# Unit samples loaded in 32x32 blocks and transposed by VectorE, unit results stored by GpSimd's queue, splitting of weights respread, 8 idle matmuls

## The chip, the core and the metric

One Trainium2 chip; the kernel runs on one core of it. The metric is device time in microseconds (us) of one execution, the median of several. The core has TensorE (matmuls), VectorE, ScalarE, GpSimd and SyncE, each with an in-order instruction stream of its own; the profile calls them PE (and PEld for its weight loads), DVE, ACT, POOL and SP. Streams wait for one another by semaphores. DMAs are issued by an engine's stream (here SP and POOL, and a few by ACT) and carried out by 16 DMA engines.

## The reference

A batch of 128 samples `x` of 64 rows by 256 columns, in float32. Every sample passes two shared two-layer networks and one of five expert networks, chosen by its integer `itok`; a gate from the samples' first rows mixes the three results; a residual and a stencil step follow. Cut to its core:

```python
def _dense(x, wi_, wo_):
    return jax.nn.relu(x @ wi_) @ wo_            # 256 -> 1024 -> 256
s0, s1 = _dense(x, swi[0], swo[0]), _dense(x, swi[1], swo[1])
h = jax.nn.relu(jnp.einsum('bsd,bdf->bsf', x, wi[itok]))
eo = jnp.einsum('bsf,bfd->bsd', h, wo[itok])
gate_in = jnp.concatenate([eo[:, 0], s0[:, 0], s1[:, 0]], axis=-1)
w = softmax(relu(gate_in @ g1) @ g2)[:, :, None, None]
x = x + eo * w[:, 0] + s0 * w[:, 1] + s1 * w[:, 2]
# then, per sample, with the scalars zX, zY, zR:
x = x + zX * lap_x(x) + zY * lap_y(x) + zR * x * (1 - x)
```

## The kernel before

**Passes and chunks.** The work of TensorE is a row of passes (PASSES), each of 8 chunks of 128 hidden columns. Passes 0 and 1 (PRE) send the samples' first rows through the two shared networks. Passes 2 to 23 (EXP) are 22 expert units: a unit is 8, 4 or 2 samples of one expert, called B, S and T here; pass n does unit n-2, and the order of sizes is BBTBBSBTBSBBTBSBSBTBSB. Which sample stands in which of the 132 slots is worked out on the chip and written into the small table `tab`. Passes 24 to 55 (SH) are 16 tiles of 8 samples times the two shared networks; the gate, the residual and the stencil are done beside them. FIRST is 24.

**A chunk on the engines.** Float32 products are made of split operands: a high part (float32r) by ScalarE and the remainder by VectorE. In step g TensorE does the first product of chunk g (six matmuls with XH, XL and the split weights into `hbank`) and the second product of chunk g-2 (LAG is 2) into `acc`. In between ScalarE makes HH (`hidden_high`, L865) and VectorE HL (`hidden_low`, L528). The second product of a chunk waits for its HL.

**The samples of a unit.** Pass n works on tile n-1. In the pass before, the tile is made ready: SP loads each sample by one DMA into XS (`load_unit_x`, L1023), in rows that lie 8, 4 or 2 partitions apart, having read the sample's number from `tab` (L1010, L1011); TensorE transposes the 128x128 blocks into the PSUM bank `tbank` (`transposes`, L721 to L726); ScalarE takes the high part (`tile_high`, L848, L851) and VectorE the remainder (`tile_low`, L458, L461). For B this is done in two halves, in chunks 3 and 6 (T_ORDER, `tile_parts`). XS has two buffers: the load of tile t waits until tile t-2 has been transposed.

**The tiles of the shared stage** are loaded otherwise: `load_tile_blocks` (L1056) lays 32x32 blocks so that VectorE's transpose, which works within 32x32 blocks, gives the whole transpose at once (`turn_tile`, L471), then `tile_high_whole` (L857) and `tile_low_whole` (L476).

**Weights and results.** GpSimd's stream issues the weights of a unit in four pieces of 512 KB (`load_unit`, L978), each when the raw buffer has been split for the unit before; `cuts_at` is the table that says in which chunk ScalarE splits which piece (L896), VectorE following one chunk later (L561). The unit's results go out by one DMA per sample (`store_unit`, L1033) in SP's stream, in turn with the loads; only half of the last unit's stores are in GpSimd's (L994).

Of the kernel before, what the change touches and what calls it, by code (L numbers as in the profile page):

```python
# [28 lines left out]
WARM = 14  # L29
# [42 lines left out]
def tile_parts(n, c):  # L72

    if n == 0 or n >= FIRST - 1:
        return []
    tile = tile_of(n) + 1
    big = UNITS[tile - 1][1] == 8
    if c == (4 if n == 1 else 3):
        return [(tile, 0 if big else None)]
    return [(tile, 1)] if c == (5 if n == 1 else 6) and big else []  # L80
# [24 lines left out]
def next_tile(n, c):  # L105

    if c != 4 or n < FIRST - 1 or n >= NP - 2:
        return None
    if n == FIRST - 1:
        return 0  # L110
    t, b = PASSES[n][1] // 2, PASSES[n][1] % 2
    return t + 1 if b == 1 else None
# [3 lines left out]


def tile_last(tile):
    return (tile, 1) if (tile, 1) in T_AT else (tile, None)
# [8 lines left out]
def cuts_at(n, c):  # L128
    out = list(FIRST_CUTS.get((n, c), ()))
    at = {2: 0, 4: 2} if 2 <= n < 1 + NU and UNITS[n - 2][1] == 2 else {2: 0, 4: 2, 5: 1, 7: 3}  # L130
    if 2 <= n < 1 + NU and c in at:
        out.append((n + 1, at[c]))

    if 3 <= n <= 1 + NU and UNITS[n - 3][1] == 2 and c < 2:
        out.append((n, 1 + 2 * c))
    return out
# [30 lines left out]
def cond_resid_program(nc, x, itok, zx, zy, zr, wi, wo, swi, swo, g1, g2, out):  # L167
    eo_d = nc.dram_tensor("eo_scratch", (NS + NSLOT, S, D), F32, kind="Internal").ap()
    ctx = ExitStack()
    with ctx:  # L170
# [14 lines left out]
        HF = sb("hf", [128, NH, 128])  # L185
        XS = [sb(f"xs{i}", [128, 4, D]) for i in range(2)]
        EO = [sb(f"eo{i}", [128, 4, D]) for i in range(2)]
        ident = sb("ident", [128, 128])
# [19 lines left out]
        S01 = sb("s01", [128, 2, D])  # L208
# [68 lines left out]
        XB, XZ = RW[0:2], RW[2]  # L277

        def unit_cols(a):
            return a[:].rearrange("p (k n) -> p k n", k=2)  # L280
# [48 lines left out]
        for tile in range(1 + NU + NT):  # L329
            x_slot[tile % 2] += 16 * (slots_of(tile - 1)[1] if 1 <= tile <= NU else 1)  # L330
            X_VAL[tile] = x_slot[tile % 2]
        st_slot = [0, 0]
        ST_VAL = {}
        for u in range(NU):
            st_slot[u % 2] += 16 * slots_of(u)[1] // (2 if u == NU - 1 else 1)
            ST_VAL[u] = st_slot[u % 2]
# [7 lines left out]
        def _(e):  # L344
# [107 lines left out]
            def tile_low(tile, k):  # L452

                hi, lo = unit_cols(XH[tile % 2]), unit_cols(XL[tile % 2])
                e.wait_ge(t_hi, XT_AT[tile, k])
                if k is None:
                    w = S * UNITS[tile - 1][1]
                    e.tensor_tensor(lo[:, :, 0:w], tbank[:, 0:2 * w].rearrange("p (k n) -> p k n", k=2),  # L458
                                    hi[:, :, 0:w].bitcast(F32), ALU.subtract).then_inc(t_free, 1)
                else:  # L460
                    e.tensor_tensor(lo[:, k, :], tbank[:], hi[:, k, :].bitcast(F32),  # L461
                                    ALU.subtract).then_inc(t_free, 1)

            def turn_tile(t):

                if t == 0:
                    e.wait_ge(*cut_done(1 + NU, 2))
                else:
                    e.wait_ge(xt_lo, t)
# [3 lines left out]
            def tile_low_whole(t):  # L473
                tile = 1 + NU + t
                e.wait_ge(xt_hi, t + 1)
                e.tensor_tensor(XL[tile % 2][:], XZ[:], XH[tile % 2][:].bitcast(F32), ALU.subtract).then_inc(xt_lo, 1)  # L476
# [212 lines left out]
        def _(e):  # L689
# [22 lines left out]
            def transposes(tile, k):  # L712
                src = XS[tile % 2]
                e.wait_ge(t_free, T_AT[tile, k] - 1)
                e.wait_ge(x_in[tile % 2], X_VAL[tile])
                if k is None:
                    js = UNITS[tile - 1][1] // 2
                    for kk in range(2):
                        for j in range(js):
                            at = (kk * js + j) * 128  # L720
                            i = e.transpose(tbank[:, at:at + 128], src[:, j, kk * 128:(kk + 1) * 128], ident[:])  # L721
                    i.then_inc(t_prod, 1)
                    return
# [13 lines left out]
            def first_product(g):  # L737
# [16 lines left out]
                if PASSES[n][0] == EXP:  # L754
                    xh, xl = ([unit_cols(a[tile % 2])[:, k, 0:w] for k in range(2)] for a in (XH, XL))
                    to = bank[:, 0:w]
                    if c == 0:
                        e.wait_ge(t_free, T_AT[tile_last(tile)])
                else:
                    xh, xl = ([tile_cols(a[tile % 2], k) for k in range(2)] for a in (XH, XL))  # L760
                    to = bank[:].rearrange("p (j n) -> p j n", j=4)
                    if c == 0:
                        e.wait_ge(xt_lo, PASSES[n][1] // 2 + 1)
# [73 lines left out]
        def _(e):  # L837
# [3 lines left out]
            def tile_high(tile, k):  # L841
                hi = unit_cols(XH[tile % 2])
                e.wait_ge(t_prod, T_AT[tile, k])
                if tile >= 3:
                    e.wait_ge(h_prod, (LAST_PASS[tile - 2] + 1) * NC)
                if k is None:
                    w = S * UNITS[tile - 1][1]
                    e.activation(hi[:, :, 0:w], tbank[:, 0:2 * w].rearrange("p (k n) -> p k n", k=2),  # L848
                                 ACT.Copy).then_inc(t_hi, 1)
                else:  # L850
                    e.activation(hi[:, k, :], tbank[:], ACT.Copy).then_inc(t_hi, 1)  # L851

            def tile_high_whole(t):
                tile = 1 + NU + t
                e.wait_ge(xz_done, t + 1)
                e.wait_ge(h_prod, (LAST_PASS[tile - 2] + 1) * NC)
                e.activation(XH[tile % 2][:], XZ[:], ACT.Copy).then_inc(xt_hi, 1)  # L857
# [40 lines left out]
            def first_samples():  # L898

                e.wait_ge(t_free, T_AT["rows"])  # L900
                e.wait_ge(dve_seq, AT["samples"])
                for b in range(1, 8, 2):
                    e.reg_load(regs[b // 2], tab[0:1, 0, b:b + 1])
                    v = e.snap(regs[b // 2], min_val=0, max_val=NS - 1)
                    e.dma_start(XS[1][b:128:8, :, :], x[bass.ds(v, 1), :, :].rearrange("a (p j) d -> (a p) j d", p=16)) \
                        .then_inc(x_in[1], 16)
# [38 lines left out]
        def _(e):  # L945
# [37 lines left out]
            load_unit(0, (3,))  # L983
            for u in range(1, NU):
                load_unit(u, (0, 2, 1, 3))


            u = NU - 1
            s0, k = slots_of(u)
            e.wait_ge(acc_free, ACC[2 + u, blocks(2 + u) - 1])  # L990
            for b in range(1, k, 2):
                e.reg_load(reg, tab[0:1, 1, s0 + b:s0 + b + 1])
                v = e.snap(reg, min_val=0, max_val=NS + NSLOT - 1)
                e.dma_start(eo_d[bass.ds(v, 1), :, :].rearrange("a (p j) d -> (a p) j d", p=128 // k),  # L994
                            EO[u % 2][b:128:k, 0:k // 2, :]).then_inc(last_out, 16)
# [10 lines left out]
        def _(e):  # L1006
# [6 lines left out]
            def load_unit_x(u, part=None):  # L1013
# [5 lines left out]
                if tile >= 3:  # L1019
# [7 lines left out]
            def store_unit(u, part=None):  # L1027
                s0, k = slots_of(u)
                n = 2 + u
                e.wait_ge(acc_free, ACC[n, blocks(n) - 1])  # L1030
                for b in part or range(k):
                    v = table_value(1, s0 + b, b % 4, NS + NSLOT - 1)
                    e.dma_start(eo_d[bass.ds(v, 1), :, :].rearrange("a (p j) d -> (a p) j d", p=128 // k),  # L1033
                                EO[u % 2][b:128:k, 0:k // 2, :]).then_inc(eo_out[u % 2], 16)

            def load_tile_x(t):
                tile = 1 + NU + t
                if t < 2:
                    e.wait_ge(t_prod, T_AT[tile_last(tile - 2)])
# [4 lines left out]
            def load_tile_blocks(t):  # L1044
# [5 lines left out]
                if t >= 2:  # L1050
                    e.wait_ge(xz_done, t - 1)
# [45 lines left out]
            for u in range(NU):  # L1097
# [6 lines left out]
                if u >= 1:  # L1104
                    store_unit(u - 1)
            store_unit(NU - 1, range(0, slots_of(NU - 1)[1], 2))
# [54 lines left out]
```

## Time and profile before

| | |
|---|---|
| time, median of 3 runs | 1160.17 us (1158.34 to 1160.6) |
| the profiled execution | 1159.52 us, of it 1158.0 us span |
| PE busy | 1135.8 us, 98% |
| DVE / ACT / POOL busy | 675.9 / 453.8 / 72.7 us |
| expert passes, from the first chunk to the first shared chunk | 29.8 to 424.4 us |
| chain that ended last | PE 97%, DVE 1%, DMA 1% |

The first section of the page gives each engine's busy time and its share of the span; the chain of waits is followed back from the last instruction, and tells which engine's work or wait the end hangs on. Instructions that issue DMAs or read registers on SP are not counted as busy; they stand in the timeline as SPq, with the time that each holds SP's stream.

### The profile page before, as it was taken

How to read it: one execution, taken by the hardware profiler on the slowest of the kernel's cores; microseconds unless marked ns; L12 is line 12 of the kernel's file. 1: busy time of each engine (PE TensorE's matmuls, PEld its weight loads, DVE VectorE, ACT ScalarE, POOL GpSimd, SP SyncE). 2: the span in 40 equal slices, each digit the busy share in tenths (PEclk: the TensorE clock that was granted, in tenths of full speed). 3: DMA queues.
4: the chain of work that ended last, by engine and by line, in shares of the span. 5: the costliest groups of instructions: out<-in, count | busy, mean ns of one | idle time of the engine just before them, and what ended most of it. 6: DMA issues, size and time to landing. Idle time of an engine off the chain costs nothing.

```text
span 1158.0 us, 16675 instructions
## 1 busy us (share of the span) xinstructions
PE 1135.8 (98%) x6000; PEld 967.0 (84%) x6000; DVE 675.9 (58%) x1023; ACT 453.8 (39%) x794; POOL 72.7 (6%) x111
## 2 busy tenths in 40 slices
PE   7999999999999999999999999999999999999995
PEld 6788888888888888888888888888888888888884
DVE  6765656656666644546656655655565565465564
ACT  2655545545555532323323333332333333333232
POOL 1111112111111100000000000000000000000001
PEclk9999999999999999999999999999999999999998
DMA  6645456546555514023022022131131231230200
GB/s 216 193 139 179 137 169 183 151 146 184 172 166 153 161 33 118 17 67 83 14 70 74 19 74 41 51 74 29 58 79 21 62 83 20 63 83 15 69 28 28
DMA packets 109986, 107.78 MB, mean 93 GB/s; under 512 B 78320, under 2 KB 86736, under 8 KB 109904
## 3 DMA queue, kind: packets, MB, share of 16 engines
q1 hardware_dynamic: 96832, 60.04, 19.3%
q0 software_dynamic: 12800, 46.41, 13.3%
q8 instruction: 48, 0.79, 0.3%
q10 hardware_dynamic: 272, 0.26, 0.1%
q14 instruction: 34, 0.28, 0.1%
HBM read 85.20 MB, written 17.04 MB: 88 GB/s over the span
## 4 chain that ended last, share of the span: by engine, by line
PE 97%; DVE 1%; DMA 1%; SPq 0%; issue 0%; ACT 0%; DVEq 0%; POOL 0%; POOLq 0%; ACTq 0%
PE acc L793 31%; PE hbank L769 16%; PE hbank L768 16%; PE acc L794 16%; PE hbank L770 16%; PE tbank L725 1%; DMA rw<-in_L_cond_wi 1%; PE acc L694 0%; DMA y<-y 0%; PE tbank L721 0%; PE tbank L726 0%; PE tbank L733 0%; PE acc L782 0%; SPq L1068 0%; DVE ss L599 0%
## 5 line engine op out<-in xcount | busy, mean ns | idle before, releaser
L528 DVE SCALAR_TENSOR_TENSOR hl<-hbank,hh 128x512 fp32r<-128x512 f32 (+2 forms) x432 | 274.2, 636 | 437.1 <-ACT hh L865 436.5
L865 ACT ACTIVATE hh<-hbank 128x512 fp32r<-128x512 f32 (+2 forms) x432 | 238.9, 553 | 597.7 <-PE hbank L770 594.9
L793 PE MATMUL acc<-swo,hh 128*128 128x512 f32 x1024 | 371.0, 397 | 0.0
L794 PE MATMUL acc<-swo,hl 128*128 128x256 f32 x1024 | 286.9, 280 | 0.0
L793 PEld LDWEIGHTS acc<-swo,hh 128*128 128x128 f32 x1024 | 192.4, 188 | 45.3 <-DVE eo L546 0.2
L768 PE MATMUL hbank<-xh,swh 128*128 128x512 f32 x512 | 202.7, 396 | 0.0
L769 PE MATMUL hbank<-xl,swh 128*128 128x512 f32 x512 | 202.4, 395 | 0.0
L794 PEld LDWEIGHTS acc<-swo,hl 128*128 128x128 f32 x1024 | 193.3, 189 | 9.9
L770 PE MATMUL hbank<-xh,swl 128*128 128x512 f32 x512 | 199.4, 389 | 0.0
L793 PE MATMUL acc<-ewo,hh 128*128 128x512 f32 x528 | 194.6, 399 | 0.3
L794 PE MATMUL acc<-ewo,hl 128*128 128x256 f32 x528 | 148.0, 280 | 0.0
L768 PE MATMUL hbank<-xh,ewh 128*128 128x512 f32 (+2 forms) x352 | 124.2, 353 | 0.0
L769 PE MATMUL hbank<-xl,ewh 128*128 128x512 f32 (+2 forms) x352 | 122.3, 347 | 0.0
L770 PE MATMUL hbank<-xh,ewl 128*128 128x512 f32 (+2 forms) x352 | 121.9, 346 | 0.0
L793 PEld LDWEIGHTS acc<-ewo,hh 128*128 128x128 f32 x528 | 99.3, 188 | 22.8 <-DVE hl L528 2.2
L768 PEld LDWEIGHTS hbank<-xh,swh 128*128 128x128 f32 x512 | 96.1, 188 | 23.8
L770 PEld LDWEIGHTS hbank<-xh,swl 128*128 128x128 f32 x512 | 96.4, 188 | 22.3
L769 PEld LDWEIGHTS hbank<-xl,swh 128*128 128x128 f32 x512 | 96.2, 188 | 10.5
L794 PEld LDWEIGHTS acc<-ewo,hl 128*128 128x128 f32 x528 | 99.6, 189 | 4.1
L768 PEld LDWEIGHTS hbank<-xh,ewh 128*128 128x128 f32 x352 | 66.4, 189 | 10.9
L770 PEld LDWEIGHTS hbank<-xh,ewl 128*128 128x128 f32 x352 | 66.4, 188 | 9.5
L769 PEld LDWEIGHTS hbank<-xl,ewh 128*128 128x128 f32 x352 | 66.8, 190 | 4.5
(169 smaller groups left out, 844.5 us busy)
## 6 DMA issues: line engine op xcount, KB each, us to landing
rw<-in_L_cond_wi POOLq DMA_DIRECT2D x44, 512.0 KB, 4.4
rw<-in_L_cond_wo POOLq DMA_DIRECT2D x44, 512.0 KB, 4.6
xs<-in_x SPq DMA_DIRECT2D x128, 64.0 KB, 3.1
eo_scratch<-eo SPq DMA_DIRECT2D x128, 64.0 KB, 2.5
xs<-in_x SPq DMA_DIRECT2D x16, 512.0 KB, 4.2
rw<-in_x SPq DMA_DIRECT2D x256, 32.0 KB, 2.2
ei<-eo_scratch SPq DMA_DIRECT2D x16, 512.0 KB, 5.5
out<-ot SPq DMA_DIRECT2D x15, 512.0 KB, 6.3
```

The costliest lines, as they stand in the source:

```text
L528: e.scalar_tensor_tensor(HL[:, g % NH, 0:w], bank[:, 0:w], 0.0, HH[:, g % NH, 0:w].bitcast(F32), ALU.max, ALU.subtract).then_inc(h_lo, 1)
L725: e.transpose(tbank[:, j * 128:(j + 1) * 128], src[:, j, k * 128:(k + 1) * 128], ident[:])
L768: e.matmul(to, wh[:, k, cs], xh[k], start=(k == 0), stop=False)
L769: e.matmul(to, wh[:, k, cs], xl[k], start=False, stop=False)
L770: i = e.matmul(to, wl[:, k, cs], xh[k], start=False, stop=(k == 1))
L793: e.matmul(acc[j][:, 0:2 * D], HH[:, g % NH, js], woc[:, c, :], start=(c == 0), stop=False)
L794: m = e.matmul(acc[j][:, D:2 * D], HL[:, g % NH, js], woc[:, c, 0:D], start=False, stop=last)
L865: e.activation(HH[:, g % NH, 0:w], hbank[g % HRING][:, 0:w], ACT.Relu).then_inc(h_hi, 1)
```

## The change

- **Loads.** From tile 3 on (the third unit) a sample of a unit is loaded by 4 DMAs of 32 partitions x 4 pieces of 32 columns (128 bytes each), so that the tile lies in 32x32 blocks. Tiles 1 and 2 are still loaded by one DMA a sample and transposed by TensorE, in another layout of rows. The load of tile t waits for VectorE's transpose of tile t-2.
- **Transposes.** From tile 3 on VectorE transposes XS into the new buffer XZ in chunk 3 of the pass before, ScalarE takes the high part of the whole tile from XZ, and VectorE the remainder in chunk 4, as in the shared stage. XZ was a part of the raw weights' buffers; now HF and S01 lie in it.
- **Stores.** All unit results are stored from GpSimd's stream, those of unit u-3 between the second and the third piece of unit u's weights (4 instead of 2 DMAs for a T unit); half of the last unit's are left on SP.
- **Splitting of weights.** `cuts_at`: a T pass splits one piece and leaves three to the next pass's chunks 0, 1, 2; an S pass two and two (chunks 0, 1); a B pass all four, some a chunk later or earlier after a T.
- **Start.** 8 instead of 14 idle matmuls (two rows each in the profile) on TensorE.

```diff
-WARM = 14
+WARM = 8
...
 def tile_parts(n, c):
+    if n == 1 and c in (4, 5):
+        return [(1, c - 4)]
+    return [(2, c // 6)] if n == 2 and c in (3, 6) else []
...
 def next_tile(n, c):
 
-    if c != 4 or n < FIRST - 1 or n >= NP - 2:
+    if c != (3 if n < FIRST - 1 else 4) or n < 3 or n >= NP - 2 or (n >= FIRST and PASSES[n][1] % 2 == 0):
         return None
...
+    return tile_of(n) + 1
...
+    if 2 <= n < 1 + NU:
+        size = UNITS[n - 2][1]
+        late = 3 <= n and UNITS[n - 3][1] == 2
+        at = {2: 0} if size == 2 else {2: 0, 4: 2} if size == 4 else {3 if late else 2: 0, 5 if late else 4: 2,
+                                                                      6 if late else 5: 1, 7: 3}
+        if c in at:
+            out.append((n + 1, at[c]))
+    if 3 <= n <= 1 + NU:
+        at = {2: {0: 2, 1: 1, 2: 3}, 4: {0: 1, 1: 3}, 8: {}}[UNITS[n - 3][1]]
+        if c in at:
+            out.append((n, at[c]))
...
+            def turn_tile(tile):
+
+                if XZ_AT[tile] > 1:
+                    e.wait_ge(xt_lo, XZ_AT[tile] - 1)
+                if tile <= NU:
                     w = S * UNITS[tile - 1][1]
...
+                    e.wait_ge(x_in[tile % 2], X_VAL[tile])
+                    e.transpose(XZ[:, 0:2 * w], XS[tile % 2][:].rearrange("p j d -> p (j d)")[:, 0:2 * w]) \
+                        .then_inc(xz_done, 1)
+                    return
...
+            def tile_low_whole(tile):
+                w = width(LAST_PASS[tile])
+                e.wait_ge(xt_hi, XZ_AT[tile])
+                e.tensor_tensor(XL[tile % 2][:, 0:2 * w], XZ[:, 0:2 * w], XH[tile % 2][:, 0:2 * w].bitcast(F32),
+                                ALU.subtract).then_inc(xt_lo, 1)
...
+            def tile_high_whole(tile):
+                w = width(LAST_PASS[tile])
+                e.wait_ge(xz_done, XZ_AT[tile])
                 e.wait_ge(h_prod, (LAST_PASS[tile - 2] + 1) * NC)
-                e.activation(XH[tile % 2][:], XZ[:], ACT.Copy).then_inc(xt_hi, 1)
+                e.activation(XH[tile % 2][:, 0:2 * w], XZ[:, 0:2 * w], ACT.Copy).then_inc(xt_hi, 1)
...
+            def store_unit(u, part=1):
+                s0, k = slots_of(u)
+                e.wait_ge(acc_free, ACC[2 + u, blocks(2 + u) - 1])
+                for i, (b, g) in enumerate(stores(u)[::part]):
+                    e.reg_load(targets[i % 4], tab[0:1, 1, s0 + b:s0 + b + 1])
+                    v = e.snap(targets[i % 4], min_val=0, max_val=NS + NSLOT - 1)
+                    to, of = store_ends(u, b, g, v)
+                    e.dma_start(to, of).then_inc(eo_out[u % 2], 16)
+
+            e.wait_ge(dve_seq, AT["targets"])
             for u in range(1, NU):
-                load_unit(u, (0, 2, 1, 3))
...
+                load_unit(u, (0, 2))
+                if u >= 3:
+                    store_unit(u - 3)
+                load_unit(u, (1, 3))
...
-                if tile >= 3:
-                    e.wait_ge(t_prod, T_AT[tile_last(tile - 2)])
+                if tile in (3, 4):
+                    e.wait_ge(t_prod, T_AT[tile - 2, 1])
+                if tile >= 5:
+                    e.wait_ge(xz_done, XZ_AT[tile - 2])
+                to = XS[tile % 2][:].rearrange("p j d -> p (j d)")[:, 0:128 * k].rearrange("p (c b n) -> p c b n", c=4, b=k)
                 for b in part or range(k):
                     v = table_value(0, s0 + b, b % 4, NS - 1)
-                    e.dma_start(XS[tile % 2][b:128:k, 0:k // 2, :],
-                                x[bass.ds(v, 1), :, :].rearrange("a (p j) d -> (a p) j d", p=128 // k)) \
-                        .then_inc(x_in[tile % 2], 16)
...
+                    rows = sample.rearrange("a (r g) (k d) -> (a r) (g k) d", g=2, k=2)
+                    for q in range(4):
+                        qs = slice(32 * q, 32 * q + 32)
+                        e.dma_start(to[qs, :, b, :], rows[:, :, qs]).then_inc(x_in[tile % 2], 16)
...
-                if u >= 1:
-                    store_unit(u - 1)
```

How the instructions stand now, at three places. First SP's stream at the load of a sample from tile 4 on. Before, two samples (TENSOR_LOAD reads the sample's number, ISA works out the address):

```order
L1010 TENSOR_LOAD tab
L1011 ISA
L1023 DMA xs<-in_x 16x1024
L1010 TENSOR_LOAD tab
L1011 ISA
L1023 DMA xs<-in_x 16x1024
```

Now, one sample and the head of the next:

```order
L1053 DMA xs<-in_x 32x4x32
L1053 ISA
L1053 DMA xs<-in_x 32x4x32
L1053 ISA
L1053 DMA xs<-in_x 32x4x32
L1053 ISA
L1053 DMA xs<-in_x 32x4x32
L1028 TENSOR_LOAD tab
L1029 ISA
```

Where one DMA stood there are four, with an address instruction ahead of each of the three further ones.

Second, VectorE around chunk 3 of pass 4 (the first T pass), where tile 4 (a B tile) is made ready; `hl<-hbank` is the hidden remainder of a chunk, `ewl<-rw` a split of weights. Before:

```order
L528 SCALAR_TENSOR_TENSOR hl<-hbank1,hh 128x128
L461 TENSOR_TENSOR xl0<-tbank,xh0 128x512
L528 SCALAR_TENSOR_TENSOR hl<-hbank2,hh 128x128
L561 TENSOR_TENSOR ewl1<-rw0,ewh1 128x2x512
L528 SCALAR_TENSOR_TENSOR hl<-hbank0,hh 128x128
```

Now:

```order
L549 SCALAR_TENSOR_TENSOR hl<-hbank1,hh 128x128
L486 STREAM_TRANSPOSE xz<-xs0 128x1024
L549 SCALAR_TENSOR_TENSOR hl<-hbank2,hh 128x128
L582 TENSOR_TENSOR ewl1<-rw0,ewh1 128x2x512
L496 TENSOR_TENSOR xl0<-xz,xh0 128x1024
L549 SCALAR_TENSOR_TENSOR hl<-hbank0,hh 128x128
```

Between the HL of chunk 2 and that of chunk 3 stands the transpose of the whole tile, and the whole remainder stands ahead of the HL of chunk 4; both stood as halves, the second half in chunk 6.

Third, GpSimd's stream: before, the four pieces of a unit's weights stood alone. Now, with three of the eight stores of a B unit:

```order
L987 DMA rw<-in_L_cond_wo 128x4x256
L999 TENSOR_LOAD tab
L1000 ISA
L1002 DMA eo_scratch<-eo 64x1x256
L999 TENSOR_LOAD tab
L1000 ISA
L1002 DMA eo_scratch<-eo 64x1x256
```

The third and the fourth piece (L987) come after the last of these stores.

## Rows read from the trace of the kernel before

**Rows 1.** First section of the page: busy time (share of span) and instructions
```profile
PE 1135.8 (98%) x6000; PEld 967.0 (84%) x6000; DVE 675.9 (58%) x1023; ACT 453.8 (39%) x794; POOL 72.7 (6%) x111
```
**Rows 2.** Two windows: us, busy (instructions) PE, PEld, DVE, ACT, POOL, clock, DMA, GB/s
```profile
1.50:3.00 1.50, 1.50 (x7) 1.50 (x8) 0.36 (x3) 1.28 (x1) 1.08 (x5) 1.00 0.47 103
...
30.00:424.40 394.40, 392.69 (x2228) 339.65 (x2227) 242.60 (x367) 208.69 (x363) 61.11 (x83) 1.00 0.53 158
```
**Rows 3.** TensorE's timeline: the first shared chunk
```profile
424.44 0.39 PE L768 MATMUL hbank<-xh,swh 128*128 128x512 f32 x1
```
**Rows 4.** SP's timeline: a B unit's loads (start us, us)
```profile
103.17 7.46 SPq L1023 DMA_DIRECT2D xs<-in_x  x8
```
**Rows 5.** TensorE's transposes of unit samples: durations ns min/median/max, first and last start
```profile
L725 PE MATMUL tbank<-ident,xs x78: 270/272/328, 24.1 to 400.4; 128*128 128x128 f32 x78
L721 PE MATMUL tbank<-ident,xs x28: 270/272/273, 61.3 to 375.8; 128*128 128x128 f32 x28
L726 PE MATMUL tbank<-ident,xs x26: 272/272/273, 24.5 to 400.5; 128*128 128x128 f32 x26
```
**Rows 6.** The chain in order of time (start us, us, what), pieces of several windows
```profile
1.48 5.33 PE acc L694 x28
...
47.09 0.33 PE tbank L725 x3
...
80.85 0.33 PE tbank L725 x3
...
84.35 0.33 PE tbank L725 x3
...
395.68 0.33 PE tbank L725 x3
396.00 0.11 PE tbank L726
...
400.33 0.33 PE tbank L725 x3
```
**Rows 7.** The chain in the window 14 to 20: one sample on SP
```profile
16.21 0.28 SPq L1010
...
16.53 0.04 SPq L1011
...
16.67 0.50 SPq L1023
17.17 0.04 issue
```
**Rows 8.** What a DMA holds SP: all unit samples; a T unit's (window 123:126); shared blocks, landing
```profile
L1023 SPq DMA_DIRECT2D xs<-in_x x128: 472/495/753, 15.5 to 378.5; - x128
...
L1023 SPq DMA_DIRECT2D xs<-in_x x2: 550/551/552, 123.5 to 124.6; - x2
...
L1056 SPq DMA_DIRECT2D rw<-in_x x16: 577/608/647, 487.1 to 497.2; - x16
...
DMA to landing us min/median/max: 2.1/2.2/2.4
```
**Rows 9.** Groups by line and form: count | busy us, mean ns of one | idle before
```profile
L471 DVE STREAM_TRANSPOSE rw<-rw 128x1024 f32<-128x1024 f32 x16 | 19.8, 1238 | 3.2 <-DMA rw<-in_x 3.2
L476 DVE TENSOR_TENSOR xl<-rw,xh 128x1024 fp32r<-128x1024 f32 x16 | 19.5, 1216 | 0.0
L857 ACT ACTIVATE xh<-rw 128x1024 fp32r<-128x1024 f32 x16 | 17.0, 1063 | 50.9 <-DVE rw L471 50.9
L528 DVE SCALAR_TENSOR_TENSOR hl<-hbank,hh 128x256 fp32r<-128x256 f32 x40 | 16.8, 420 | 13.9 <-ACT hh L865 13.9
L865 ACT ACTIVATE hh<-hbank 128x256 fp32r<-128x256 f32 x40 | 15.3, 384 | 24.0 <-PE hbank L770 23.4
```
**Rows 10.** GpSimd's timeline: the first and the last of its four stores
```profile
432.52 0.53 POOL L994 DMA_DIRECT2D eo_scratch<-eo  x1 [38.35 <-issue]
...
435.78 0.48 POOL L994 DMA_DIRECT2D eo_scratch<-eo  x1 [0.42 <-issue]
```

More of the change, by code:

```diff
@@ L105, in next_tile @@
 def next_tile(n, c):
-    if c != 4 or n < FIRST - 1 or n >= NP - 2:
+    if c != (3 if n < FIRST - 1 else 4) or n < 3 or n >= NP - 2 or (n >= FIRST and PASSES[n][1] % 2 == 0):
         return None
[L109 to L112, printed above, removed]
+    return tile_of(n) + 1
+XZ_AT = {}
+for _n, _c in CHUNKS:
+    if next_tile(_n, _c) is not None:
+        XZ_AT[next_tile(_n, _c)] = len(XZ_AT) + 1
 LAST_PASS = {tile_of(n): n for n in range(NP)}
-def tile_last(tile):
-    return (tile, 1) if (tile, 1) in T_AT else (tile, None)
 FIRST_CUTS = {(0, 4): [(0, 0)], (0, 5): [(0, 2)], (0, 6): [(0, 1)], (0, 7): [(0, 3)], (1, 3): [(2, 0)], (1, 6): [(2, 2)],
@@ L329, in cond_resid_program, with stores, store_ends @@
         for tile in range(1 + NU + NT):
-            x_slot[tile % 2] += 16 * (slots_of(tile - 1)[1] if 1 <= tile <= NU else 1)
+            x_slot[tile % 2] += 16 * (slots_of(tile - 1)[1] * (1 if tile <= 2 else 4) if 1 <= tile <= NU else 1)
             X_VAL[tile] = x_slot[tile % 2]
+        def stores(u):
+            return [(b, g) for b in range(slots_of(u)[1]) for g in ((0, 1) if slots_of(u)[1] == 2 else (None,))]
+        def store_ends(u, b, g, v):
+            ps, js = unit_rows(u, b, g or 0)
+            to = eo_d[bass.ds(v, 1), :, :].rearrange("a (r g) d -> (a r) g d", g=2)
+            return to if g is None else to[:, g:g + 1, :], EO[u % 2][ps, js, :]
         st_slot = [0, 0]
@@ L334, in cond_resid_program @@
         for u in range(NU):
-            st_slot[u % 2] += 16 * slots_of(u)[1] // (2 if u == NU - 1 else 1)
+            st_slot[u % 2] += 16 * len(stores(u)) // (2 if u == NU - 1 else 1)
             ST_VAL[u] = st_slot[u % 2]
@@ L715, in transposes @@
                 e.wait_ge(x_in[tile % 2], X_VAL[tile])
[L716 to L723, printed above, removed]
                 for j in range(3):
@@ L754, in first_product @@
                 if PASSES[n][0] == EXP:
[L755 to L758, printed above, removed]
+                    xh, xl = ([unit_cols(a[tile % 2], k, w) for k in range(2)] for a in (XH, XL))
+                    to = bank[:, 0:w].rearrange("p (g n) -> p g n", g=2)
+                    if c == 0 and tile <= 2:
+                        e.wait_ge(t_free, T_AT[tile, 1])
+                    elif c == 0:
+                        e.wait_ge(xt_lo, XZ_AT[tile])
                 else:
@@ L983, in _ @@
             load_unit(0, (3,))
-            for u in range(1, NU):
-                load_unit(u, (0, 2, 1, 3))
[L988 to L995, printed above, removed]
+            targets = [e.alloc_register(f"target{k}") for k in range(4)]
+            def store_unit(u, part=1):
[7 more added lines that the diff above has]
+            e.wait_ge(dve_seq, AT["targets"])
+            for u in range(1, NU):
+                load_unit(u, (0, 2))
+                if u >= 3:
+                    store_unit(u - 3)
+                load_unit(u, (1, 3))
+            store_unit(NU - 3)
+            store_unit(NU - 2)
+            store_unit(NU - 1, 2)
             t = NT - 1
```

92 lines of the change are left out of this document (35 added, 57 removed).

## The prediction

> **What bounds the kernel now.** I read the busy times first. TensorE is busy for 1135.8 of 1158.0 us [rows 1], and the chain that ended last is TensorE for 97% (the table). So one asks of every edit only whether TensorE has less to do, or comes to wait. Then the expert passes as a window: from 30.0 to 424.4 us TensorE is busy for 392.7 of 394.4 us, VectorE for 242.6, ScalarE for 208.7, GpSimd for 61.1 [rows 2]. Nothing but TensorE's work sets the length of this stage, and the shared stage behind it, from 424.44 us on [rows 3], isn't touched but for its first tile. The whole question is when the first shared chunk starts.
>
> SP is in none of these shares, since an instruction that issues a DMA isn't counted as busy. Its timeline has to be read: the eight loads of a B unit hold its stream for 7.46 us [rows 4], so a sample costs (7.46 - 0.50)/7 = 0.99 us. With 116 loads from the third unit on and nearly as many stores that is about 230 us of the stage's 394: SP has room. This is the number that the change moves most.
>
> **What TensorE is spared.** It transposes 78 + 28 + 26 = 132 blocks [rows 5]; the 16 of tiles 1 and 2 stay, 116 go. Their durations overlap; on the chain four of them take 0.33 + 0.11 = 0.44 us [rows 6], 0.11 each. Sum: 12.8 us, all on the path, as nothing else bounds it there. The idle matmuls: 28 rows take 5.33 us from 1.48 us on [rows 6], the first ones 1.50/7 = 0.214 us each [rows 2]. The 16 that are left end at 1.48 + 3.42 = 4.9 us instead of 6.8, and the table of slots, on which the first weights wait, follows: 1.9 us. If the slower pace of the first rows then lasts longer, a part is given back, at worst all 5.33 us that the idle matmuls took; between -1.9 and +5 us, and I take -1.9. With no new wait at all the profiled execution would be 1159.5 - 14.7 = 1144.8 us.
>
> **What SP has to do now.** Stores leave it (they cost 116 us of a stream that wasn't bound, so nothing). A load becomes four DMAs. The anatomy of one sample before [rows 7]: from the address instruction to the DMA 0.14 us (16.53 to 16.67), behind it 0.04 us, and the reading of the number in front. The three further DMAs each bring an address instruction and themselves: 0.18 + d, where d is what such a DMA holds the stream. The first costs 0.50 + d, by the 0.99 us above with d = 0.495. A sample is 1.04 + 4d.
>
> d isn't in the trace. The rows around it [rows 8]: the lowest of all unit loads 0.472 us (no loads by register are cheaper), 64 pieces of 1 KB by register 0.551 us, and the shared tiles' blocks, 32 partitions x 8 pieces of 128 bytes at constant addresses, 0.608 us. The new DMA has the form of the last with half the pieces, and an address from a register; the bounds are 0.47 (the lowest row) and 0.68 (the highest, and on it the 0.08 by which small pieces by register exceed the lowest). I take 0.58, between the two nearest rows. A sample then costs 3.36 us, a B unit 26.9, an S unit 13.4, a T unit 6.7.
>
> TensorE needs less: three chunks of an S pass take 400.33 - 395.68 - 0.44 = 4.21 us and three of a T pass 84.35 - 80.85 - 0.44 = 3.06 us [rows 6], so 1.40 and 1.02 a chunk, and a B chunk, with twice an S chunk's columns, 2.79; a B pass is about 20 to 22 us. SP falls behind by up to 5 us with each B unit. Only two buffers lie between them, so it becomes the bound.
>
> The ledger. Tile 4, from which SP is never idle again by these numbers, may be loaded when the second half of tile 2 is transposed, before at 47.09 + 0.44 = 47.5 us [rows 6], now 45.6. From there 22 tiles less three, 114 samples x 3.36 = 383.0 us: tile 22, the last, is issued at 428.6 us. Its landing takes 2.2 us [rows 8]. Then, in pass 22 (S), stand in line VectorE's transpose 1.24, ScalarE's high part 1.06 and hidden high part 0.38, VectorE's hidden remainder 0.42, a split of weights and the remainder of the tile 1.22 each, and the hidden remainder of chunk 4, 0.42 [rows 9]: 5.96 us, to 436.8. There TensorE goes on with the second product of chunk 4, which stands 3 x 1.40 + 0.70 = 4.9 us behind the start of chunk 3. From the start of chunk 3 to the first shared chunk it took 424.44 - 395.68 - 0.88 (two transposes) = 27.9 us [rows 3, 6], so 23.0 are left: the first shared chunk starts at 459.8 us, 35.4 later than before. The first shared tile's 16 DMAs at 0.65 us (0.608 + 0.04) follow tile 22 and are there before chunk 4 of pass 23. The sum against the execution's own time: 1159.5 + 35.4 = 1194.9 us; that execution lies 0.7 us below the median of the runs, which is less than I can tell, so 1195.
>
> The Trainium skill, in DMA: Bandwidth & Descriptors, "Issuing engines are not separate DMA queues", says that the time on the sequencer to start a DMA is "usually small relative to the DMA itself". By that rule the queue wouldn't bound and the time would be that of the first rival below; the trace disagrees for these pieces, as four of 16 KB would each hold the stream for 0.76 us where the old one of 64 KB held it for 0.99 in all.
>
> **The other edits.** Results through GpSimd: its stores lie (435.78 - 432.52)/3 = 1.09 us apart [rows 10], so eight hold back the third and fourth piece of weights by 8.7 us, about three B chunks. A store of unit u-3 isn't needed before pass u. The pieces come about a pass ahead, so I cost it at nothing while SP stretches the passes; without that, up to 2 us behind each of the four T units, 8 in all. VectorE's added transposes (11 B, 5 S, 4 T tiles, at most 1.24 each: 17 us) fit into its 150 idle us, except where they stand ahead of a hidden remainder in a short pass (below). The respread splitting moves no work; it keeps four splits of 1.22 us out of a T pass of 10 us. I cost it at nothing.
>
> **The rivals.** First, SP keeps up: d is at or below 0.47, a sample at or below 2.93 us. Then tile 22 is issued by 45.6 + 334 = 379.6 us, ahead of chunk 3 of its pass, and the time is 1145 us, the full 14.7 gained. For it: one row at 0.472. Against it: all rows with small pieces are above 0.55. This is the other side.
>
> Second, SP keeps up, but the gain goes into the new line through VectorE and ScalarE in the short passes. In a T pass it is, from the start of chunk 3, 0.3 (VectorE comes to it late by a hidden remainder) + 1.24 + 1.06 + 0.28 + 0.29 + 1.22 + 1.22 + 0.29 = 5.9 us to the remainder of chunk 4, against 3 x 1.02 + 0.67 = 3.7 in which TensorE needs it: 2.2 us, four times. In an S pass 6.3 against 4.9: 1.3 us, five times. (The 128-column forms are taken as two thirds of the 256-column ones.) Together 15 us, so 1160 us: no change. The line holds whether or not SP is late; with SP late it is hidden but for the last, which the ledger has.
>
> Third, SP bound and dearer: d = 0.608 gives 3.47 us a sample, 1159.5 + 48 = 1207; d = 0.68 gives 1240. Cheaper: 0.551 gives 1182. Every 0.01 us of d is 4.6 us of time. Fourth, the transfers don't do what they should: pieces of 128 bytes beside the weights land late. With 2.2 us landing against a pass of lead this costs a few us at most, and it is in the range.
>
> **How the numbers follow.** SP bound with d from 0.52 to 0.64, the forecast and what lies around it (1166 to 1222 us): 0.62. Dearer still: 0.10. SP keeps up, with the gain kept or partly kept (1145 to 1157): 0.18. SP keeps up or nearly, with nothing gained: 0.10, most of it within 0.2%. The likeliest case's own range is 1170 to 1220. The range that holds 8 in 10 reaches down to 1150 and up to 1226. About 0.2% (2.3 us) is what a measurement of this kernel can tell from no change: faster 0.20, within it 0.07, slower 0.73.
>
> **What would show it.** Right: in the changed profile SP's stream has no idle time between the loads from tile 4 to 22; a B unit holds it for about 27 us; VectorE's transpose of unit tiles is what TensorE's chain passes through, with the loads (DMA, SPq) as its releaser, tiles 5, 11, 12, 16, 18 and 22 most; TensorE is busy for some 14 us less and idle for some 50 us in the expert passes, and the shared stage is as long as before. Wrong: SP waits for VectorE's transposes (then it kept up), or TensorE's waits end on ScalarE's high part without a late DMA (second rival), or on weights whose DMA GpSimd issued behind its stores; or the time is under 1165.

## The result and the profile after

The changed kernel takes 1204.3 us, median of 4 runs (1202.88 to 1207.21), against 1160.38 us (1158.34 to 1160.71) before: ratio 1.0385, interval 1.0362 to 1.0409. It is slower by 44 us; the prediction said 1195 us, slower with a chance of 0.73. The page of the changed kernel, busy times and chain:

```profile
PE 1143.8 (95%) x5872; PEld 969.2 (81%) x5872; DVE 690.6 (57%) x1032; ACT 451.1 (38%) x783; POOL 141.2 (12%) x243
...
PE 64%; SPq 28%; issue 5%; DMA 1%; DVE 1%; ACT 0%; DVEq 0%; POOL 0%; ACTq 0%; POOLq 0%
SPq L1053 24%; PE acc L808 21%; PE acc L809 11%; PE hbank L783 11%; PE hbank L784 11%; PE hbank L785 10%; SPq L1028 3%; SPq L1029 0%; DMA xs<-in_x 0%; DMA rw<-in_L_cond_wi 0%; PE acc L715 0%; DMA y<-y 0%; PE tbank L746 0%; PE acc L797 0%; PE hbank L763 0%
```

Where TensorE had 97% of the chain, SP's issuing has 28% of it now. The expert stage as a window up to the first shared chunk, which answers to the second row of [rows 2] and to [rows 3] (the columns are those of rows 2):

```profile
30.00:468.38 438.38, 398.97 (x2106) 340.78 (x2105) 255.87 (x376) 205.68 (x351) 129.55 (x215) 0.95 0.54 141
```

The first shared chunk starts at 468.38 us instead of 424.44, 43.9 later, and from there to the end of the span it takes 733.8 us (before 733.6): all of the loss lies in the expert stage. TensorE is idle for 39.4 us of it (before 1.7). And it is *busy* for 6.2 us more than before, though it transposes 116 blocks fewer: the granted clock of the window is 0.95 instead of 1.00. The two sum to the 43.9.

The line of the loads and their landing; SP's timeline over 12 samples (start us, us):

```profile
L1053 SPq DMA_DIRECT2D xs<-in_x x457: 563/563/1835, 39.9 to 432.4; - x153
...
DMA to landing us min/median/max: 1.9/2.7/6.6
```
```profile
204.97 40.48 SPq L1053 DMA_DIRECT2D xs<-in_x  x48
```

One of these DMAs holds SP for 563 ns, a sample for 40.48/12 = 3.37 us where it took 0.99. A merged row of SP's timeline would hide idle time, so the row itself doesn't show that there is none; the sum does: 12 samples by the prediction's formula with d = 0.563 are 39.5 of the 40.5 us. In the trace no two neighbouring instructions of SP lie more than 0.4 us apart from the first load of tile 4 (46.26 us) to the last issue. SP never catches up. Who waited, on VectorE and on TensorE (us in total, times, longest):

```profile
DVE xz L486 <- DMA xs<-in_x: 30.6, 5, 9.3
```
```profile
PE acc L808 <- DVE hl L549: 32.7, 15, 7.3
PE acc L808 <- DVE ewo L582: 4.7, 4, 1.2
```

VectorE's transpose waits five times for a tile, 30.6 us in all: for tiles 5, 11, 12, 18 and 22, five of the six that the prediction named (16 came in time). TensorE's waits are put down to the hidden remainder (L549), which stands behind that transpose in VectorE's stream; the DMA is found one step further back. The longest of the five in windows of TensorE (columns as in rows 2):

```profile
234.00:238.00 4.00, 4.00 (x22) 3.37 (x21) 0.59 (x1) 0.00 (x0) 1.23 (x2) 1.00 0.62 154
238.00:242.00 4.00, 2.19 (x11) 1.49 (x10) 0.00 (x0) 0.00 (x0) 0.00 (x0) 1.00 0.50 149
242.00:246.00 4.00, 0.00 (x0) 0.00 (x0) 1.25 (x1) 0.84 (x1) 0.00 (x0) 0.53 0.12 19
246.00:250.00 4.00, 2.52 (x8) 2.15 (x9) 3.27 (x4) 3.56 (x6) 0.71 (x1) 0.50 0.14 21
250.00:254.00 4.00, 4.00 (x16) 3.29 (x15) 2.56 (x4) 0.60 (x1) 1.30 (x2) 0.69 0.84 165
```

TensorE stands still from about 240 to 247 us; the granted clock falls to half (0.50: 1.2 of 2.4 GHz) in the stall and is still there while TensorE works again: 22 matmuls in a full window at 1.00, 16 in the one at 0.69. Whether that is paid for depends on what is late next: where the next tile comes late anyway, a slower TensorE only waits less.

The end of the stage: SP's last loads, VectorE's last unit transpose, TensorE behind it.

```profile
425.83 7.14 SPq L1053 DMA_DIRECT2D xs<-in_x  x9
```
```profile
437.98 1.25 DVE L486 STREAM_TRANSPOSE xz<-xs 128x1024 f32<-128x1024 f32 x1 [5.14 <-DMA xs<-in_x]
```
```profile
441.10 0.79 PE L808 MATMUL acc<-ewo,hh 128*128 128x512 f32 x1 [4.91 <-DVE hl L549]
```

The last issue ends at 432.97, the tile is there 5.0 us later, and the first matmul behind it takes 0.79 us instead of 0.4.

### The profile page after: what moved, and what is told of

Read it like the earlier page. It is cut to its first block, busy times and chain, and to the rows that moved or that the text cites. A ratio compares the mean times of both kernels' runs of the same rounds, so it can differ in the third digit from the quotient of the medians.

```text
span 1202.2 us, 17512 instructions
## 1 busy us (share of the span) xinstructions
PE 1143.8 (95%) x5872; PEld 969.2 (81%) x5872; DVE 690.6 (57%) x1032; ACT 451.1 (38%) x783; POOL 141.2 (12%) x243
## 4 chain that ended last, share of the span: by engine, by line
PE 64%; SPq 28%; issue 5%; DMA 1%; DVE 1%; ACT 0%; DVEq 0%; POOL 0%; ACTq 0%; POOLq 0%
SPq L1053 24%; PE acc L808 21%; PE acc L809 11%; PE hbank L783 11%; PE hbank L784 11%; PE hbank L785 10%; SPq L1028 3%; SPq L1029 0%; DMA xs<-in_x 0%; DMA rw<-in_L_cond_wi 0%; PE acc L715 0%; DMA y<-y 0%; PE tbank L746 0%; PE acc L797 0%; PE hbank L763 0%
## 5 line engine op out<-in xcount | busy, mean ns | idle before, releaser
L549 DVE SCALAR_TENSOR_TENSOR hl<-hbank,hh 128x512 fp32r<-128x512 f32 (+2 forms) x432 | 273.6, 636 | 456.7 <-ACT hh L873 456.2
L808 PE MATMUL acc<-ewo,hh 128*128 128x512 f32 x528 | 202.9, 413 | 38.0 <-DVE hl L549 32.7
L808 PEld LDWEIGHTS acc<-ewo,hh 128*128 128x128 f32 x528 | 102.5, 194 | 64.3 <-DVE hl L549 36.5
L809 PE MATMUL acc<-ewo,hl 128*128 128x256 f32 x528 | 151.1, 286 | 0.0
L784 PE MATMUL hbank<-xl,ewh 128*128 128x512 f32 (+2 forms) x352 | 125.9, 358 | 0.0
L785 PE MATMUL hbank<-xh,ewl 128*128 128x512 f32 (+2 forms) x352 | 125.3, 356 | 0.0
L809 PEld LDWEIGHTS acc<-ewo,hl 128*128 128x128 f32 x528 | 103.1, 195 | 4.2
L1002 POOL DMA_DIRECT2D eo_scratch<-eo x136 | 69.5, 511 | 96.4 <-issue 84.2
L783 PEld LDWEIGHTS hbank<-xh,ewh 128*128 128x128 f32 x352 | 69.8, 198 | 13.1
```

Source lines behind the costliest of these rows:

```text
L549: e.scalar_tensor_tensor(HL[:, g % NH, 0:w], bank[:, 0:w], 0.0, HH[:, g % NH, 0:w].bitcast(F32), ALU.max, ALU.subtract).then_inc(h_lo, 1)
L783: e.matmul(to, wh[:, k, cs], xh[k], start=(k == 0), stop=False)
L784: e.matmul(to, wh[:, k, cs], xl[k], start=False, stop=False)
L785: i = e.matmul(to, wl[:, k, cs], xh[k], start=False, stop=(k == 1))
L808: e.matmul(acc[j][:, 0:2 * D], HH[:, g % NH, js], woc[:, c, :], start=(c == 0), stop=False)
L809: m = e.matmul(acc[j][:, D:2 * D], HL[:, g % NH, js], woc[:, c, 0:D], start=False, stop=last)
```

## Experiments

The theory after this reading: the loss is SP's issuing of four DMAs a sample (A). What was open: whether the number of DMAs, their duration, or the small pieces and their late landing decide it; what the other edits cost once SP keeps up; and what the clock adds.

**One DMA a sample, in before's form.** All other edits stay.

```diff
-                    for q in range(4):
-                        e.dma_start(to[qs, :, b, :], rows[:, :, qs])...
+                    e.dma_start(XS[tile % 2][b:128:k, 0:k // 2, :],
+                                sample.rearrange("a (p j) d -> (a p) j d", p=128 // k))...
...
```

> The changed kernel, but from tile 3 on each unit sample is loaded by one DMA in the form of the kernel before (pieces of 4, 2 or 1 KB); all waits, VectorE's transposes, GpSimd's stores and the table of splits stay. The rows are not laid out for a 32x32 transpose, so the values of the expert passes are other ones. Theory (SP's issuing bounds the expert passes): SP needs 0.99 us a sample instead of 3.4, VectorE never waits for xs, and about 50 us of the 44 lost and 15 gained come back: 1145 to 1157 us, the first shared chunk at 410 to 422 us. Rival 1 (the new line through VectorE and ScalarE in S and T passes costs as much as the transposes did): 1160. Rival 2 (GpSimd's queue holds the weights back and is what TensorE waits for): stays above 1190.

Measured: 1171.83 us (ratio 1.0101, 1.0086 to 1.0117). The stage, and TensorE's waits:

```profile
30.00:436.22 406.22, 388.77 (x2103) 332.49 (x2102) 254.75 (x374) 205.32 (x350) 129.14 (x215) 0.98 0.51 151
```
```profile
PE acc L808 <- DVE hl L549: 10.8, 13, 1.2
PE acc L808 <- DVE ewo L582: 4.7, 4, 1.2
```

32.5 us of the 44 go with the three further DMAs: A holds for them. But the time lies in neither expected range (1145 to 1157, or 1160): the kernel is still 12 us slower than before where 14.7 us of gain were due. SP isn't waited for any more, and yet TensorE is idle for 17.4 us, and busy for 9.5 us longer than in the version further down whose clock never falls in this window (379.3). Here the granted clock is at half for 17.1 us of the window, in four stretches, one in each T pass. So there are further causes, of 27 us together.

**Four DMAs with one piece of 512 bytes a partition.** The same number of DMAs, bytes and partitions, larger pieces.

```diff
-                        e.dma_start(to[qs, :, b, :], rows[:, :, qs])...
+                        e.dma_start(whole[qs, 128 * b:128 * b + 128],
+                                    rows[:, q:q + 1, :].rearrange("r o d -> r (o d)"))...
```

> The changed kernel with its four DMAs a sample, each to 32 partitions by register as now and of the same 16 KB, but in one piece of 512 bytes a partition instead of four of 128. The pieces land in another arrangement, so the values of the expert passes are other ones. Theory (the number of issues on SP bounds): d stays at 0.50 to 0.57 us, the loads end at 410 to 433 us and the time is 1180 to 1205. Rival (it is the pieces of 128 bytes that make the transfers slow and late): 1145 to 1165, as with one DMA a sample.

Measured: 1171.44 us (1.0072 to 1.0105). What a DMA holds SP:

```profile
L1054 SPq DMA_DIRECT2D xs<-in_x x464: 315/316/1468, 33.9 to 393.7; - x155
```

The expectation that d stays near 0.5 us failed: it is 0.316. So the run doesn't separate pieces from issuing as it was meant to. It shows something else: the count of DMAs alone doesn't bind, but the count times what each holds SP for. By the prediction's formula a sample is 1.04 + 4 x 0.316 = 2.3 us, SP keeps up, and the time is that with one DMA.

**The start alone.** The kernel before, `WARM = 8`.

> The kernel before with 8 instead of 14 idle matmuls and nothing else. Theory: the first shared chunk comes 1.3 us earlier, as the first chunk of pass 2 does in the changed kernel (28.5 against 29.8 us): 1159.1 us. Rival (the small matmuls behind stay at half speed for longer and give it back, or the slot table isn't what the first weights wait for): 1160.4, no change.

Measured: 1157.34 us against 1159.66 (ratio 0.9979, 0.997 to 0.9988): 2.3 us faster (1.4 to 3.5), more than the 1.3 expected here. In the profiled execution the first shared chunk starts at 422.55 us, 1.9 earlier:

```profile
30.00:422.55 392.55, 390.83 (x2220) 338.21 (x2220) 241.32 (x365) 207.82 (x361) 61.06 (x83) 1.00 0.52 157
```

The windows all begin at 30 us, so a version that starts earlier has that much less work in them: 390.8 us busy is what the 392.7 of before become by the start alone.

**One DMA a sample in 32x32 blocks.** The pieces of 128 bytes and their places stay as in the changed kernel; the four column groups are one dimension of the source.

```diff
-                    for q in range(4): ...
+                    src = sample.rearrange("a (r g) (k q d) -> (a q) r (g k) d", g=2, k=2, q=4)
+                    e.dma_start(to[:, :, b, :], src).then_inc(x_in[tile % 2], 16)
...
```

> The changed kernel, but a sample's four DMAs are put into one, with a source pattern of 4 column groups x 32 rows x 4 x 32 columns onto all 128 partitions: 512 pieces of 128 bytes, the same layout and the same values. Theory (issues on SP bound, not the pieces): a sample costs SP at most 1.3 us, no stall for samples is left, 1145 to 1160 us. Rival (the pieces bound, or such a pattern runs on few of the 16 DMA engines and lands late): VectorE waits for xs as now, 1170 to 1230.

Measured: 1172.53 us (1.0093 to 1.0124). The DMA, and the stage:

```profile
L1052 SPq DMA_DIRECT2D xs<-in_x x116: 577/584/3557, 33.4 to 386.3; - x116
```
```profile
30.00:437.30 407.30, 389.30 (x2105) 332.82 (x2104) 255.58 (x376) 205.42 (x351) 129.54 (x215) 0.98 0.57 151
```

The time is that of 4 KB rows within 0.7 us. The small pieces as transfers cost the kernel nothing that can be measured; SP's time at four DMAs a sample does. With the runs before, this settles A: the time comes back with fewer DMAs of the same pieces, and with as many that hold SP for less.

It missed both expectations, though: 1172.5 isn't in 1145 to 1160, and VectorE doesn't wait for xs as the rival had it. Nor is a sample as cheap as the row's median (0.584) suggests. SP's timeline at a B unit's loads, then at the sixth and seventh of them alone; and the reading of the number (ns, min/median/max):

```profile
97.18 16.65 SPq L1052 DMA_DIRECT2D xs<-in_x  x8
```
```profile
104.87 6.29 SPq L1052 DMA_DIRECT2D xs<-in_x  x2
```
```profile
L1028 SPq TENSOR_LOAD <-tab x132: 263/736/924, 13.8 to 447.9; - x132
```

The first five DMAs of the unit take 0.58 us each, the last three 1.7 to 3.1. Over all 116 the mean is 1.05 us, 44 of them take more than 0.6, and reading the number takes 0.74 us where it took 0.27. So a sample costs SP 2.0 us on average, twice that of 4 KB rows (0.99) and more than the 1.3 expected; with four DMAs it is 3.4. That is still little enough: SP has some 120 idle us left. Why the later ones of a unit take longer isn't shown.

**The transpose earlier in short passes.** Theory B: the line VectorE, ScalarE, VectorE in S and T passes is what is left. Its start is moved up, VectorE's transpose to chunk 0 and ScalarE's high part to chunk 2, first with four DMAs a sample, then with one block DMA.

```diff
+def turn_next(n, c):
+    if short(n):
+        return tile_of(n) + 1 if c == 0 else None
+    return next_tile(n, c)
+def high_next(n, c):
+    if short(n):
+        return tile_of(n) + 1 if c == 2 else None
+    return next_tile(n, c)
```

> The changed kernel with its four DMAs a sample, but in the S and T passes VectorE's transpose of the next tile stands in chunk 0 and ScalarE's high part in chunk 2 instead of both in chunk 3; the remainder stays in chunk 4. Theory (SP's issuing bounds, the line through VectorE and ScalarE costs only where SP is not late): the loads end at 433 us as now, tile 22's transpose now blocks VectorE from chunk 0 on, so nothing is won: 1200 to 1208 us. Rival (the stalls of the short passes, and the clock that falls with them, are a loss of their own beside SP's): 1175 to 1190.

Measured with four DMAs: 1204.87 us (ratio 1.0398, 1.0382 to 1.0414), as without it. The stage, and TensorE's waits:

```profile
30.00:468.43 438.43, 392.45 (x2102) 336.09 (x2101) 253.61 (x374) 205.55 (x350) 129.10 (x215) 0.96 0.53 140
```
```profile
PE acc L824 <- DVE eo L579: 26.4, 6, 7.1
PE acc L824 <- DVE hl L565: 13.4, 5, 5.6
```

The stage is as long to 0.05 us, but otherwise made up: busy 392.5 instead of 399.0 us, idle 46.0 instead of 39.4. What TensorE saves at a better clock it waits for. While SP is late, neither VectorE's line nor, but for the last tile, the clock moves the end.

> One block DMA a sample as in e4, and the transpose in chunk 0 and the high part in chunk 2 of the S and T passes as in e5. Theory (of the 12 us that e4 still loses, the line through VectorE's transpose, ScalarE's high part and VectorE's remainder in chunks 3 and 4 of the short passes is the larger part, with the clock that falls behind the 1.6 us stalls of the T passes): TensorE's waits for hl fall from 10.8 to under 2 us, the clock stays up but for about the first 16 us, the 4.7 us for the split of wo stay; 1150 to 1156 us. Rival (the clock falls with any of the other waits, the one for wo included): 1158 to 1168.

Measured with one block DMA: 1155.88 us (0.9962 to 0.9982), 16.6 us less than with the block DMA alone. The stage:

```profile
30.00:421.53 391.53, 379.27 (x2102) 325.30 (x2101) 253.92 (x374) 205.77 (x350) 129.22 (x215) 1.00 0.59 157
```

Against the same window without the early transpose, idle time falls from 18.0 to 12.3 us and busy time from 389.3 to 379.3: 5.7 us are waits, 10.0 us the clock, which stays at full speed in the whole window. The waits for the hidden remainder fall from 10.8 to 3.2 us, not to under 2 as expected; the 4.7 for the split stay. The same edit is worth nothing or 16.6 us, by what else is late.

The first T pass shows where the clock goes. With one DMA and the late transpose, the chain (start us, us), then TensorE's windows:

```profile
78.14 0.29 ACT hh L873
78.48 0.17 issue
78.66 1.25 DVE xz L486
80.04 0.15 issue
80.20 0.69 issue
80.89 0.27 ACT hh L873
81.18 0.29 DVE hl L549
81.47 1.13 DVE ewl L582
82.61 1.14 DVE xl L496
83.74 0.21 DVE hl L549
84.00 0.80 PE acc L808
```
```profile
80.00:84.00 4.00, 2.41 (x19) 2.03 (x18) 2.82 (x5) 1.76 (x5) 0.71 (x1) 0.95 0.89 298
84.00:88.00 4.00, 4.00 (x13) 3.52 (x14) 0.63 (x3) 0.28 (x1) 0.00 (x0) 0.50 0.46 149
88.00:92.00 4.00, 4.00 (x15) 3.23 (x14) 0.69 (x1) 1.78 (x3) 0.00 (x0) 0.70 0.00 0
92.00:96.00 4.00, 2.81 (x14) 2.07 (x13) 3.61 (x5) 3.04 (x5) 0.90 (x2) 1.00 0.02 4
```

With the early transpose and the splits of the next experiment, the same pass:

```profile
82.00:86.00 4.00, 3.21 (x19) 2.72 (x19) 2.65 (x6) 0.60 (x3) 1.99 (x3) 1.00 0.83 264
86.00:90.00 4.00, 3.92 (x19) 2.97 (x18) 2.36 (x4) 3.79 (x6) 1.63 (x5) 1.00 0.79 209
```

The wait that ends at 84.00 (1.23 us, another of 0.36 ahead of it) is followed by matmuls at half clock up to the window from 88; 0.79 us of idle time in the fastest version isn't. By the clock's column, nor is the wait for the split, 1.19 us in the window from 92. It is the same in all four T passes of this execution, and none of the single waits of 0.9 us in S passes is followed by half clock. That the two waits so close together bring the clock down is read from this, not tested by itself. The Trainium skill, in TensorE: Matmul & The Clock Gate, "Part 1: The HAM clock gate", says that "the default state is throttled, and activity releases the throttle". The trace agrees: the half clock outlasts the wait, and comes back to 1.00 while TensorE works.

**The old table of splits after T passes.** The piece with the second weights is split in the T pass again.

```diff
-        at = {2: 0} if size == 2 else {2: 0, 4: 2} if size == 4 else {3 if late else 2: 0, ...
+        at = {2: 0, 4: 2} if size <= 4 else {3 if late else 2: 0, ...
-        at = {2: {0: 2, 1: 1, 2: 3}, 4: {0: 1, 1: 3}, 8: {}}[UNITS[n - 3][1]]
+        at = {2: {0: 1, 1: 3}, 4: {0: 1, 1: 3}, 8: {}}[UNITS[n - 3][1]]
```

> As e6, and a T pass splits two pieces (chunks 2 and 4) and leaves two to the next pass, as the kernel before did, instead of one and three. Theory (the respread table is what makes TensorE wait 4.7 us for the split of wo): that wait goes, VectorE has the room in the T pass since the transpose is out of chunk 3; 1144 to 1150 us, 10 to 15 us below the kernel before. Rival (VectorE gets too full in the T passes with two splits, a transpose and a remainder): as e6 or slower.

Measured with block DMA and early transpose: 1149.26 us against 1159.59 (ratio 0.9915, 0.9901 to 0.9928), the fastest version; it beats the kernel before by 10.3 us and the changed one by 55. Its stage, and the longest wait left:

```profile
30.00:413.45 383.45, 378.50 (x2103) 325.29 (x2101) 254.07 (x374) 204.54 (x350) 129.33 (x215) 1.00 0.60 160
```
```profile
PE acc L824 <- DVE hl L565: 3.2, 4, 0.9
```

> The kernel after with one DMA a sample (as in the block load by one DMA, 1172.5 us) and only the table of splits put back for T passes: the piece that holds the second weights is split in chunk 4 of the T pass, not in chunk 0 of the next one. VectorE's transpose stays in chunk 3. Theory A, the waits for the split (4.7 us in four places) and the half clock behind them are a cost of their own: the waits for the split are gone, those for the hidden remainder stay near 10.8 us, and the time is 1164 to 1168 us. Theory B, the split only changes places in the line of the T pass: it now stands between the tile's transpose and its remainder there, so the waits for the hidden remainder grow by what the others lose, and the time is 1171 to 1176 us. In the kernel with the early transpose the same edit gave 6.6 us, which tells nothing on that line.

Measured with the block DMA and the late transpose: 1165.57 us (1.0033 to 1.0061), 7.0 less than 1172.53. Theory A of this expectation holds as to the waits: the one for `ewo` is gone, and that for the hidden remainder is what it was:

```profile
PE acc L808 <- DVE hl L549: 10.7, 13, 1.2
```
```profile
30.00:431.33 401.33, 388.90 (x2104) 332.70 (x2103) 256.01 (x376) 205.20 (x351) 129.09 (x215) 0.98 0.58 153
```

Its second half, a half clock behind the waits for the split, doesn't hold: idle time falls from 18.0 to 12.4 us, but busy time only from 389.3 to 388.9, and the clock is at half for 17.1 us in either window. The ten runs of this version spread from 1160.23 to 1167.12 us, the four shortest, up to 1164.64, with the higher mean clock (0.992 to 0.993, the others 0.988 to 0.989): what the clock takes here differs from run to run by some us, even of one kernel.

So the new table costs about 7 us with either place of the transpose (6.6 and 7.0).

**Stores behind all four pieces of weights.** In the fastest version:

```diff
                 load_unit(u, (0, 2))
+                load_unit(u, (1, 3))
                 if u >= 3:
                     store_unit(u - 3)
-                load_unit(u, (1, 3))
```

> The fastest kernel so far (block load by one DMA, early transpose, old table after T passes: 1149.3 us) with GpSimd's stores of a unit's results behind the fourth piece of the weights and not between the second and the third. Theory A, the stores hold back nothing that TensorE waits for, since the pieces come about a pass ahead: 1148.5 to 1150 us, the first waits of ScalarE for weights (2 to 3 us, hidden) gone. Theory B, the stores in front of the third and fourth piece cost up to 2 us behind each T unit, 8 in all: 1141 to 1147 us.

Measured: 1149.57 us (0.9898 to 0.9931), no difference. That GpSimd's stores stand in the middle of the weights costs TensorE nothing here. (Their move from SP to GpSimd was in every version since the change and wasn't tested by itself.)

## Why the prediction was right, and where it was off

**What bounds the kernel: right.** SP's stream, which no busy share shows. It has no idle time from tile 4 to tile 22, and the experiments with one DMA a sample take 32 us away. The rival in which SP keeps up isn't what happened.

**TensorE spared: right.** 12.8 us were worked out. The fastest version, at full clock, is busy for 378.5 us, against 390.8 in the kernel before with the same start: 12.3 less. (Against the kernel before itself, 392.7, a part of the difference is the start.) In the changed kernel itself nothing of this is seen, since 399.0 - 379.3 = 19.7 us, what matmuls at half clock take longer, lie over it. "TensorE is busy for some 14 us less" was therefore wrong, and so was "idle for some 50 us" (39.4).

**The start: right.** -1.9 us was taken, -2.3 measured alone. In the changed kernel's profile the first chunk of pass 2 starts 1.3 us earlier than before (28.16 against 29.45).

**A sample on SP: right.** d was taken as 0.58, measured 0.563; a sample as 3.36, measured (432.97 - 46.2)/114 = 3.39. The formula gives 3.29 with the measured d; of the 11 us that this leaves open over 114 samples, single long DMAs (up to 1.84 us) are some 7. The lower bound of d, taken from the cheapest load by register [rows 8], was none: another form holds SP for 0.316.

**The ledger: 8.6 us short**, 35.4 for 43.9. Last issue at 433.0 instead of 428.6: 4.4, most of it the 0.03 us a sample, 114 times. Landing 5.0 instead of 2.2 us: 2.8; the row taken was that of shared blocks [rows 8], and landings of unit samples reach 6.6 us in the row above. From VectorE's transpose to the first shared chunk 30.4 instead of 29.0: 1.4. The line through VectorE and ScalarE isn't where they come from: the second product of chunk 4 starts 5.85 us behind the start of the transpose, worked out as 5.96. TensorE's timeline and the window from there:

```profile
443.83 0.67 PE L808 MATMUL acc<-ewo,hh 128*128 128x512 f32 x1
```
```profile
444.00:448.00 4.00, 4.00 (x18) 3.57 (x17) 1.87 (x3) 0.77 (x2) 0.00 (x0) 0.62 0.32 50
```

The clock is still at half there, for about 3 us more, which is 1.5 us of work. The mechanism is that of the prediction; the mis-sized terms are the sample on SP (3.39 for 3.36, 114 times), the last landing, and the missing term for the clock at the end.

**The other edits.** The stores at nothing: right as to their place among the weights, also without SP as a cover, where up to 8 us had been allowed. The respread splitting at nothing: wrong. The step failed in "it keeps four splits of 1.22 us out of a T pass": the table before had only two of the next unit's four pieces there (0 and 2, in chunks 2 and 4), the new one has one. What moves is the split of piece 2, and it moves to the first chunk of the next pass, where TensorE waits for `ewo` 1.2 us, four times, and the edit costs 7 us once SP keeps up. What it costs in the changed kernel itself, behind SP, wasn't measured apart.

**VectorE's line in short passes.** The second rival's 5.9 us from chunk 3 to the remainder of chunk 4 in a T pass is 84.00 - 78.14 = 5.86 in the trace. The waits that follow were put at 15 us and are 10.8 (0.36 + 1.23 in a T pass for 2.2, 0.86 in an S pass for 1.3). But the time for "SP keeps up, line eats gain", 1160, is 1172 in three experiments. Most of the difference is the wait for the splits, 4.7, and the half clock behind the T passes' waits, 9.5 us, less the 4 us by which the line was put too high: two terms that stood in no case. That the forecast came out near all the same rests on SP being the bound, which covers them. Had d been below 0.47, the forecast for that case would have been wrong by 12 us or more, and the first rival's 1145 by 27.

So the 44 us lie in layers: a gain of 14.7 us; over it the line, the splits and the clock behind them, which make 11 to 12 us of loss out of it (25.0 us by the three terms); and over these SP, with 32.5 us more, which hides them. The fastest version has 10.3 us of the gain. What it still lacks, 4.4 us, is 3.2 us of waits for the hidden remainder in the T passes, by the row above; the rest wasn't followed up.

## What to carry to other kernels

Before one DMA is made into several, work out what an issue holds its queue for and multiply by the count: SP had 160 idle us of 394 and still became the bound at four issues a sample (3.4 us), while the same 512 pieces in one DMA cost 2.0 us a sample. Read more than the median of what an issue takes: the one DMA's median was 0.58 us, its mean 1.05. When a bound is removed, look for the lines that it covered, and price each wait of a microsecond on TensorE twice, as idle time and as a possible stretch at half clock behind it. An edit that wins nothing beside a bound may be worth 16 us without it, so test it again.

## What the runs showed of the hardware

- What an issue holds SP for isn't set by bytes. Medians: 0.316 us for 32 partitions x one piece of 512 bytes and 0.563 for 32 x 4 pieces of 128 bytes, both 16 KB; 0.495 for 16 x 4 KB and 0.584 for 128 x 4 x 128 bytes, both 64 KB. Four pieces a partition instead of one cost 0.25 us; four times the partitions 0.02 in the median, but there the mean is 1.05 (up to 3.56), and the reading of a register ahead of it goes from 0.27 to 0.74 us.
- A destination of 128 partitions with the source's four column groups as a dimension was one DMA, with no loss in the kernel's time against 4 KB rows (1172.53 and 1171.83 us), where SP had idle time left.
- Waits of 0.36 and 1.23 us, 2.5 us apart, were followed by half of TensorE's granted clock in all four T passes with one DMA a sample; the stage's matmuls were 9.5 us longer than in the version without. Single waits of 0.9 us (S passes) and of 1.2 us (for the splits) were not followed by it.
